# Decay tiles of a state-space scan: four steps in a ring of three instead of two steps in a ring of six

## The reference, cut to what matters

```
dt = clip(softplus(xc @ dt_W + dt_b), DT_MIN, DT_MAX)      # (8, 512, 256)
def step(h, ins):                                          # h: (8, 256, 64)
    x_t, dt_t, B_t, C_t = ins
    dA = exp(dt_t[..., None] * A)
    h = dA * h + dt_t[..., None] * B_t[:, None, :] * x_t[..., None]
    y_t = einsum('ben,bn->be', h, C_t)
```

## Time and profile before

| | |
|---|---|
| median of 3 runs | 1047.95 us (1047.13 to 1048.22) |
| the profiled execution's own time | 1046.38 us |
| its span in the trace | 1044.6 us |
| busy: PE, DVE, ACT, POOL | 941.4, 911.8, 902.2, 824.3 us |
| mean granted TensorE clock | 0.981 of full |
| scan | from about 165 to 1018 us |
| bytes moved by DMA | 337.39 MB, 268 MB of them decay tiles |
| transfers of decay tiles | 512 of 512 KB |

### The profile page before, as it was taken

The page is one execution under the profiler, slowest core; times in us unless marked ns, Lnnn a source line. Parts: engine busy times, 40 slices in busy tenths (PEclk is TensorE's granted clock), DMA queues, the critical chain, the costliest instruction groups (busy, mean ns, idle before and its releaser), DMA issues.

```text
span 1044.6 us, 24920 instructions
## 1 busy us (share of the span) xinstructions
PE 941.4 (90%) x8006; PEld 423.2 (41%) x8006; DVE 911.8 (87%) x1966; ACT 902.2 (86%) x1061; POOL 824.3 (79%) x1159
## 2 busy tenths in 40 slices
PE   5999984669999999999999999999999999999997
PEld 3566541123434343434333333434343434343436
DVE  5788965899999999999999999999999999999982
ACT  1766876799999999999999999999999999999981
POOL 5365325899898988898989888888888888989880
PEclk9999996799999999999999999999999999999999
DMA  6265479999999999999999999999999998999940
GB/s 180 79 232 214 166 256 368 365 370 373 372 348 387 341 376 355 372 351 380 346 376 354 371 353 378 351 372 342 384 348 382 344 384 327 389 342 385 351 147 11
DMA packets 86447, 337.39 MB, mean 323 GB/s; under 512 B 15536, under 2 KB 39984, under 8 KB 50992
## 3 DMA queue, kind: packets, MB, share of 16 engines
q1 hardware_dynamic: 86288, 335.70, 86.7%
q10 hardware_dynamic: 32, 0.10, 0.0%
HBM read 308.48 MB, written 27.26 MB: 321 GB/s over the span
## 4 chain that ended last, share of the span: by engine, by line
PE 58%; DVE 16%; POOL 11%; issue 8%; ACT 3%; DMA 2%; SPq 1%; DVEq 0%; POOLq 0%; ACTq 0%
PE ps L817 17%; PE ps L902 11%; PE ps L762 9%; POOL decayed L621 9%; DVE state L1272 8%; DVE ps L1263 5%; PE ps L916 5%; PE ps L669 5%; PE ps L698 3%; PE ps L888 2%; PE ps L880 2%; PE ps L710 1%; POOL f_nrm L633 1%; DMA decay<-dt_stage 1%; DVE h L1354 1%
## 5 line engine op out<-in xcount | busy, mean ns | idle before, releaser
L621 POOL TENSOR_TENSOR decayed<-decay,state 128x256 f32<-128x256 f32 x1024 | 732.4, 735 | 107.9 <-DVE state L1272 82.9
L1035 ACT ACTIVATE decay<-decay,a_col 128x2048 f32<-128x2048 f32 x256 | 515.4, 2013 | 8.9 <-DMA decay<-dt_stage 8.9
L1272 DVE TENSOR_TENSOR state<-decayed,ps 128x256 f32<-128x256 f32 x1024 | 417.7, 417 | 40.4 <-POOL decayed L621 25.5
L1263 DVE TENSOR_TENSOR ps<-decay,ps 128x512 f32<-128x512 f32 x512 | 354.1, 692 | 26.9 <-PE ps L762 9.0
L817 PE MATMUL ps<-state,c_cols 128*32 128x256 f32 x4096 | 331.5, 396 | 2.2 <-issue 0.2
L1047 ACT COPY state<-ps 128x512 f32<-128x512 f32 x512 | 291.2, 594 | 48.5 <-issue 42.2
L762 PE MATMUL ps<-moving,b_rows 64*128 64x256 bf16 x1024 | 200.0, 276 | 64.8 <-DVE ps L1263 61.2
L769 PE MATMUL ps<-moving,b_rows 64*128 64x256 bf16 x1024 | 202.4, 279 | 10.3 <-DMA b_rows<-b_stage 10.3
L902 PE MATMUL ps<-h,w 128*128 128x256 f32 x512 | 172.4, 422 | 0.8 <-DVE h L1354 0.8
L762 PEld LDWEIGHTS ps<-moving,b_rows 64*128 64x128 bf16 x1024 | 59.9, 94 | 230.7 <-issue 138.4
L817 PEld LDWEIGHTS ps<-state,c_cols 128*32 128x32 f32 x4096 | 81.7, 108 | 113.2 <-issue 104.1
(11 more groups left out here) (118 smaller groups left out, 761.8 us busy)
## 6 DMA issues: line engine op xcount, KB each, us to landing
decay<-dt_stage SPq DMA_DIRECT2D x512, 512.0 KB, 6.2
moving<-u_stage SPq DMA_DIRECT2D x64, 256.0 KB
u_stage<-u_parts SPq DMA_DIRECT2D x16, 512.0 KB, 3.1
b_rows<-b_stage SPq DMA_DIRECT2D x64, 128.0 KB
b_stage<-b_parts SPq DMA_DIRECT2D x16, 384.0 KB, 3.0
dt_stage<-dt_tok SPq DMA_DIRECT2D x8, 512.0 KB, 3.9
moving<-u_stage SPq DMA_DIRECT2D x126, 32.0 KB
x_tok<-in_L_attn_x_dram SPq DMA_DIRECT2D x4, 512.0 KB, 4.5
```

The source lines that it names most:

```text
L621: nc.gpsimd.tensor_tensor(decayed[:, p], decay[:, dec_slot(m, k), p, k % TS, :], state[:, (k - 1) % RING, p * E:(p + 1) * E], ALU.mult).th ...
L1035: nc.scalar.activation(pair, pair, ACT.Exp, scale=a_col[:, 2:3]).then_inc(decay_ready, 1)
L1263: nc.vector.tensor_tensor(ps[:, acc_bank(m, k), :].rearrange("p (q e) -> p q e", q=HQ), decay[:, dec_slot(m, k), HQ:Q, k % TS, :], ps[:, a ...
L1272: nc.vector.tensor_tensor(state[:, k % RING, p * E:(p + 1) * E], decayed[:, p], ps[:, SELFP + k % 2, p * E:(p + 1) * E], ALU.add).then_inc ...
```

## The change

Three constants. The ring still holds 12 steps, 96 KB of each partition.

```
-    TS = 2
-    NDEC = 6
+    TS = 4
+    NDEC = 3
     NACC = 3
     BTS = STEPS // TS
-    EARLY = 2
+    EARLY = 1
```

## The result

| | before | changed |
|---|---|---|
| median of 6 runs each | 1047.71 us | 1103.28 us (1097.38 to 1109.62) |
| ratio, 95% interval | | 1.0531 (1.0514 to 1.0547) |
| profiled execution, its span | 1046.38, 1044.6 us | 1105.86, 1104.0 us |
| ACT idle until a decay tile landed | 8.9 us | 87.6 us |

The change costs 55.6 us, 5.3%. The direction was forecast, the size was not: 1070 us was named, and the range ended at 1094.

A forecast was written before the change was run, and what follows sets the result against it. PE and ACT were taken to lack slack at each scan body's end. The profiled 1046.4 us plus 20 (1.3 a body, 15 bodies) and 2.4 for the start gave 1068.8, plus 1.6 to the median: 1070 us, 8-in-10 range 1047 to 1094.

The forecast's parts named there:

- What bounds the kernel: In the scan, PE and ACT both lack slack at each body's end, so a late ACT makes the scan late.
- What is removed: Half of the decay transfers, 256 issues of SP beside the scan, with bytes and other engines' instructions unchanged; priced at 0.
- faster rival: Decay transfers with 16 KB rows run at 407 GB/s instead of 365; 1039 us at best, likelier 1043 to 1045; chance 0.10.
- The deadline: A tile's load, issued after step 4C-9, must land all 2 MB before ACT's first exponential; 8.3 and 8.1 us available.
- The time of 2 MB: Landing time of a whole decay tile without backlog: 8.3 us taken, between 8.1 and 8.5, plus 0.1 for the issue.
- The backlog behind row groups: Queue delay b of a tile behind row groups: 0.7 us for tile 72, 0.3 for tile 71; bounds 0 and 2.2.
- The other tiles of a body: Six tiles where ACT has 3 us of play; 0.2 us a body together, bounds 0 and 0.8.
- The two priced tiles: Tiles 71 (steps 284 to 287) and 72 (288 to 291): exponential 0.4 and 1.0 us late, body losing about 0.8.
- The start: Before the scan's first steps, the exponentials wait for whole 2 MB tiles; +2.4 us in full, bounds 1.5 and 3.
- The clock: If PE's pauses took the granted clock down from 1.00, the loss would exceed any sum in the prediction; no size given.
- Hidden after all: Rival: 2 MB land within 8.0 us of issue at tile 72 too, leaving only the start; 1050.4 us, chance 0.15.
- The queue saturates: Rival: the DMA queue is full, tiles near groups land 10.5 us after issue; 1089 us, up to 1100, chance 0.13.

The follow-up runs named there:

- Run 4: Changed kernel with ACT's copy of step k-2 put before the exponential of k+2 and k+3; 1071.88 us, ratio 1.0233.
- Run 3: Kernel before, with tiles issued in pairs at the later mark and ACT waiting for both tiles of a pair; 1118.18 us, ratio 1.0656.
- runs 9: Changed kernel with only the four small transfers of each row group carrying a sixteenth of their bytes; 1084.21 us, ratio 1.0352.
- 10: Changed kernel with only the two large transfers of each row group carrying a sixteenth of their bytes; 1080.51 us, ratio 1.0298.
- 13: Changed kernel with each row group's small transfers made 16 rows of a quarter length, same bytes; 1090.00 us, ratio 1.0405.
- run 5: Changed kernel with all transfers of the bodies' row groups carrying the rows of 1 step instead of 16; 1065.60 us, ratio 1.0170.
- run 6: Changed kernel with a ring of four tiles instead of three and silu_z in bf16; 1052.94 us, ratio 1.0051.
- 7: Kernel before with a ring of eight tiles instead of six and silu_z in bf16; 1046.90 us, ratio 0.9992.

## Why the prediction was right, and where it failed

**What bounds the kernel: right.** PE and ACT without slack at the end of a body, L1263 behind ACT's copy, no engine that forgives a stall. Run 4 shows the copy's part, the changed profile the two waits in a row.

**What is removed: priced at 0, in fact a gain.** Run 3 against the changed kernel gives 0.7 to 1.2% for the larger rows and fewer transfers, which this sum left out. It is the mechanism of the faster rival, and far too small to decide.

**The deadline: right.** From the release by step 4C-9 to the first exponential there were 7.8 to 8.9 us; run 3 shows that the late release and the whole tile together make the loss without any new size.

**The time of 2 MB: about right.** I took 8.3; the least disturbed tiles land at 7.5, and with thin groups at 8 to 9.

**The backlog behind row groups: this step failed.** I took b = 0.7 us for tile 72, 0.3 for tile 71 and 0 elsewhere, with a group at 1.1 us of the queue, its 480 KB by the full rate. The table of landings has 1.3 to 3 us more than the quiet tile at seven of eight places. By the skew reading a group costs its slowest engines 48 KB, not 480/16 = 30 KB (runs 9, 10 and 13). And I chose badly between the bounds: from the upper one (2.2 us, read from a landing 10.5 us after its issue) I stepped down because SP would issue the group earlier. The landings at steps 28 and 0, 9.6 and 10.1 us from the release where I had 8.7 and 9.1, say that most of it is still before the tile. An estimate from these numbers: a tile with a group takes 4.8 us and 48/64 of 2.4, 1.8 us, together 6.6, more than the 6.1 to 6.3 us from mark to mark, so the backlog passes on to the next tiles.

**The other tiles of a body: this term failed most.** "I give them 0.2 together" rested on ACT's 3 us of play. ACT waits 3.7 us a body for these six, most at the tile of step 16 (24.0 us over 14 bodies, where the tile of step 28 has 5.9 and was to have the most together with that of step 0). The two priced tiles came out as priced, at 0.4 and 1.1 us, but partly because a stall at the tile of step 24 had by then moved the next exponential too (9.6 us from the release to the exponential of step 28, 8.3 before the change). For a whole body the prediction had 1.3 us. The measured loss is 3.7 on average over the fifteen bodies behind the first (54.9 us by the starts of L1263), and 3.0 in the body at full clock; run 5 alone takes 38 us away, about 2.5 a body.

**The start: right at step 3, short for the body.** +2.4 us were forecast for step 3. ACT and DVE of the changed kernel, to be held against 170.47 and 173.05 in the earlier trace rows:

```profile
173.09 2.00 ACT L1035 ACTIVATE decay<-decay,a_col 128x2048 f32<-128x2048 f32 x1 [5.12 <-DMA decay<-dt_stage]
...
175.66 0.70 DVE L1263 TENSOR_TENSOR ps<-decay,ps 128x512 f32<-128x512 f32 x1 [3.16 <-ACT state L1047]
```

+2.6 us for both. But L1263 of step 32 is 4.6 us late (227.55 against 222.92): the first body loses more than the start, and the sum had nothing for the rest of it. In run 6, where later tiles have more lead, the 2.3 us at step 3 shrink to 0.9 by step 32, so the start's lateness doesn't always show in full either.

**The clock: named, not priced.** The text said that a fall would cost more than any sum there. It was granted at half for 3 to 7 us at a time in five bodies, which are 2 us longer. No run here keeps PE busy through the stalls, so how much of the loss is the clock's stays an estimate, some 8 to 9 us in the slower executions: the three runs with the higher clock still lose over 50 us.

**The rivals.** "Hidden after all" fell, and with it the estimate by the fit of the Trainium skill ("DMA: Bandwidth & Descriptors", "Anatomy of one DMA"): 6.8 us for 2 MB, where the least disturbed took 7.5. "The queue saturates" is nearest in size (1089 to 1100 named, 1103 measured) and half right in its mechanism. Its lump "leaves the queue empty and then behind": the share fell from 0.98 to 0.93 and 343 GB/s in the body at full clock, and by single microseconds the rate swings between 500 GB/s (890 to 891 us) and 213 (873 to 874). Its landings of 10.5 us after the issue near groups are nearer to the 9.5 to 10.1 measured at steps 28, 0 and 16 than the forecast's 8.3 with its backlog. What doesn't hold is that 0.98 was a full queue: runs 6 and 7 move the same bytes at nearly the old pace with a share of 0.93 to 0.96.

## What to carry to other kernels

The cover of a load is the time from its release to its first use less the time of all that must land, including what stands before it in the queue; count it from the release that the code really waits for. Fewer and larger tiles in the same ring cut it from both ends, and each cut may cost little alone. Price what is queued ahead of a load by its slowest DMA engine, not by its bytes over 16, and if an upper bound was read off a trace, don't step down from it without a row. And price every tile of a body: a stall that is foreseen at one place moves the others.

## What was unexpected of the hardware

Transfers of 4 rows, 96 KB of a group's 480, cost the tiles behind them as much as the other 384 KB: 19 against 23 us (runs 9 and 10), and over 16 rows they cost 13 us less (run 13). Pauses of 1.5 to 2.4 us in PE's work went with falls of the granted clock to 0.50, as from 481 to 487 us, in a scan that had kept 1.00 with pauses of 1.3.
